# Hyperbolic attention as one program: projections and unit loop share one block, spike logits ride on v's projection, GpSimd spreads v

## The reference, cut to what matters

```python
importance = sigmoid(einsum('btc,c->bt', x, w_sur) + b_sur)
spikes = importance > threshold                    # one 0 or 1 for each token
q, k, v = x @ W_qkv + b_qkv
tq, sq = expmap0(q)    # nomin = sqrt(max(-u0^2 + sum(u[1:]^2), 1e-8)); cosh(nomin), sinh(nomin) u[1:] / nomin
tk, sk = expmap0(k)
neg_inner = tq tk^T - sq sk^T
dist = arccosh(max(neg_inner, 1 + 1e-7))
attn = softmax(causal(-dist**2 / sqrt(D))) * spikes
y = (attn @ v) @ W_out + b_out
```

## Time and profile before

| what | us |
|---|---|
| median of 3 runs (2066.55 to 2072.94) | 2069.12 |
| the profiled execution, whole | 2071.58 |
| its span, first to last instruction | 2069.8 |
| the stage's first instruction (ScalarE, L1703) starts | 1114.21 |
| the first unit's stretch starts | 1169.18 |
| the next stage's first instruction starts | 1286.41 |

### The profile page before, as it was taken

One profiled execution on the slowest core, in us unless ns is written; L12 is line 12 of the kernel. 1 busy time (PEld: TensorE's weight loads), 2 busy tenths in 40 slices (PEclk: granted clock), 3 DMA queues, 4 the chain that ended last, 5 costly groups with the idle time before them and its releaser, 6 DMA issues. The chain is left out here.

```text
span 2069.8 us, 35351 instructions
## 1 busy us (share of the span) xinstructions
PE 1923.5 (93%) x12240; PEld 1620.3 (78%) x12240; DVE 1434.9 (69%) x2398; ACT 1105.4 (53%) x2118; POOL 849.8 (41%) x854
## 2 busy tenths in 40 slices
PE   8999999999999999999998677999999768959998
PEld 6788888888888888888887465788799646849998
DVE  7777676767767676776776896433589577857776
ACT  6555555545555554555544697232355365636664
POOL 7350321405032140504200185220399225968885
PEclk9999999999999999999999799999999779969999
DMA  4101010010101001010102201310156215556661
GB/s 155 62 1 62 1 61 0 20 41 0 61 0 61 0 23 37 0 61 0 29 1 62 62 3 42 123 41 11 63 192 211 65 26 148 185 204 209 213 214 45
DMA packets 96322, 144.51 MB, mean 70 GB/s; under 512 B 15358, under 2 KB 72608, under 8 KB 96096
## 3 DMA queue, kind: packets, MB, share of 16 engines
q1 hardware_dynamic: 89168, 127.21, 19.1%
q0 software_dynamic: 4928, 12.86, 1.8%
q10 hardware_dynamic: 2128, 3.15, 0.4%
HBM read 111.46 MB, written 14.16 MB: 61 GB/s over the span
## 5 line engine op out<-in xcount | busy, mean ns | idle before, releaser
L319 PE MATMUL ps<-cond_x_lo,cond_w_hi 128*128 128x512 f32 x1008 | 392.6, 389 | 0.0
L471 ACT ACTIVATE cond_h_hi<-cond_h 128x512 fp32r<-128x512 f32 x288 | 174.0, 630 | 289.7 <-DVE cond_h L666 289.6
L805 POOL TENSOR_TENSOR cond_w_lo<-cond_stage_up,cond_w_hi 128x512 fp32r<-128x512 f32 x36 | 47.1, 1308 | 591.8 <-ACT cond_w_hi L471 591.8
L319 PE MATMUL ps<-cond_x_hi_first,cond_w_hi 128*128 128x512 f32 x578 | 230.1, 398 | 3.1 <-DVE ps L652 2.5
L382 PE MATMUL ps<-cond_h_hi,cond_d_hi 128*128 128x512 f32 x576 | 224.8, 390 | 4.1 <-DVE cond_h_lo L671 4.1
L319 PE MATMUL ps<-cond_x_hi_first,cond_w_lo 128*128 128x512 f32 x578 | 225.2, 390 | 0.0
L382 PE MATMUL ps<-cond_h_hi,cond_d_lo 128*128 128x512 f32 x576 | 224.3, 389 | 0.0
L382 PE MATMUL ps<-cond_h_lo,cond_d_hi 128*128 128x512 f32 x576 | 224.2, 389 | 0.0
L319 PEld LDWEIGHTS ps<-cond_x_lo,cond_w_hi 128*128 128x128 f32 x1008 | 189.3, 188 | 37.2
L649 DVE TENSOR_TENSOR ps<-cond_p_row,ps 128x512 f32<-128x512 f32 x142 | 98.7, 695 | 170.7 <-PE ps L319 170.7
L524 ACT ACTIVATE cond_h<-ps 128x512 f32<-128x512 f32 x216 | 124.7, 596 | 164.8 <-DVE cond_h_lo L671 132.2
(11 more groups left out here) (427 smaller groups left out, 5122.4 us busy)
## 6 DMA issues: line engine op xcount, KB each, us to landing
moe_stage_up<-in_L_ffn_expert_wv SPq DMA_DIRECT2D x22, 1024.0 KB, 7.9
typed_stage_up<-in_L_cond_wi SPq DMA_DIRECT2D x11, 1024.0 KB, 5.0
typed_stage_dn<-in_L_cond_wo SPq DMA_DIRECT2D x11, 1024.0 KB
moe_stage_dn<-in_L_ffn_expert_proj SPq DMA_DIRECT2D x11, 1024.0 KB
cond_stage_up<-in_L_cond_Wg SPq DMA_DIRECT2D x7, 1024.0 KB, 5.1
cond_stage_up<-in_L_cond_Wu SPq DMA_DIRECT2D x7, 1024.0 KB, 7.2
cond_stage_dn<-in_L_cond_Wd SPq DMA_DIRECT2D x7, 1024.0 KB, 9.5
rope_v_now<-rope_v_blk SPq DMA_DIRECT2D x16, 272.0 KB, 2.4
```

Of the source, the lines that this page charges most:

```text
L319: ins = pe.matmul(bank, ws[:, j, u, w], xs.rearrange("p o n -> p (o n)"), start=(opens and k == 0), stop=(k == 2), skip_group_check=True)
L471: copy = lambda dst, src: act.activation(dst, src, ACT.Copy)
L805: return pool.tensor_tensor(w_lo[:, j, :, A11:A12 + 1], raw_up[:, :, :, upper(j)], w_hi[:, j, :, A11:A12 + 1], ALU.subtract)
```

## The change

The two programs become one block in `hyper_attention`; `hyper_units` is gone.

- The loop over the 16 projections now runs, behind the projection of block `i`, the loop's step `i - 11` (`DELAY` = `FIRST` + 4 = 11) on TensorE, ScalarE and VectorE. So steps 0 to 4 stand among the projections of blocks 11 to 15, and the loop goes on at step 5 (`AFTER`) behind them.
- The chain of the map's factors is computed for 7 blocks (`FIRST`, parts behind blocks 7 to 10) and for 9 (its parts behind the last projection and in steps 5 and 6; its exponentials on ScalarE behind step 5). The reciprocal is gone: the factors scale the features 1 to 15 of each head, and the time part is written as half a cosh.
- `stretch` scales in place, 480 columns instead of 512, by GpSimd for units 0 to 6 and by VectorE from unit 7 on.
- `block_values`, the spreading of v, goes from ScalarE to GpSimd: a multiplication by a column of ones and zeros (tile 0 and 1 ahead of the first unit, tile 2 in steps 1 and 2, tile 3 behind the phases of steps 5 and 6).
- The spike weight vector is appended, twice, to v's weights, and its bias to v's bias, so v's projection has 258 columns and the 256 small matmuls are gone. Each tile's logits get their exponential on ScalarE; the rest runs in step 6; then SP moves the spikes from token order to unit order with 8 transfers of 32 x 8 single floats. The first division (unit 0, step 8) waits for them.
- The first source tile is rounded and split in pieces of 128 and 384 tokens.
- Buffers are laid over one another: the rounded source over the residual's place, so the residual is loaded behind the last projection; the squares, the masked distances, the probabilities and y over others.

The diff, cut to its core (the phases that only change their names or places are left out):

```diff
-            self.bias, self.bo, self.ws = sb("bias", [P, 2 * D]), sb("bo", [P, KC]), sb("ws", [P, KC])
-            self.vb = sb("vb", [P, D])
+            self.bias, self.bo = sb("bias", [P, 2 * D]), sb("bo", [P, KC])
+            self.vb = sb("vb", [P, D + 2])
...
+        if b_qkv is not None:
+            self.loads += [(self.wq[:, :, 3 * D + j], col(w_sur)) for j in range(2)]
...
+                sp.wait_ge(v_done, NP)
+                sp.dma_start(resT[:].rearrange("p c n -> p (c n)"), m.x_saved).then_inc(m.x_back, 16)
+                sp.wait_ge(sp_steps, 3)
+                for q in range(2):
+                    for sq in range(4):
+                        row = sq % 2 * T + q * S
+                        sp.dma_start(spike[sq * S:(sq + 1) * S].rearrange("p (i q) -> p i q", q=2)[:, :, q],
+                                     sig[row:row + S].rearrange("p (i a) -> p i a", a=2)[:, :, sq // 2],
+                                     allow_slow_non_contiguous=True).then_inc(spike_moved, 16)
...
+                def unit_steps(u):
+                    units(u, (out, 9), (mix, 8), (score, 3), (p_turn, 7), (y_turn, 8), (turn, 1))
...
+                for i in range(NP):
+                    project(i)
+                    unit_steps(i - DELAY)
+                for u in late_steps:
+                    unit_steps(u)
...
+                for u_step in late_steps:
+                    unit_steps(u_step)
+                    if u_step == AFTER:
+                        exponentials(1)
...
+                space_norm(NP - 1)
+                norms(1, 0)
+                for u_step in late_steps:
+                    unit_steps(u_step)
+                    if u_step == AFTER:
+                        norms(1, 1)
+                        norms(1, 2)
+                    elif u_step == AFTER + 1:
+                        norms(1, 3)
+                        spikes()
...
-                        ins = act.activation(vo, vi, ACT.Copy, scale=half2[:, h:h + 1])
+                    ins = pool.tensor_scalar(vo, vi, half2[:, h:h + 1], None, ALU.mult)
...
+                for tt in range(TT - 2):
+                    for h in range(2):
+                        block_values(tt, h)
+                for u_step in range(0, AFTER):
+                    unit_steps(u_step)
+                    if u_step in (1, 2):
+                        block_values(TT - 2, u_step - 1)
+                pool.wait_ge(src_ready, TT + 1)
+                pool.memset(prob[:, 0, :, S:], 0.0).then_inc(cleared, 1)
+                for u_step in late_steps:
+                    unit_steps(u_step)
+                    if u_step in (AFTER, AFTER + 1):
+                        block_values(TT - 1, u_step - AFTER)
```

More of the change, by code:

```diff
@@ L1360, in hyper_units @@
     causal = [m.const[:, at:at + n].unsqueeze(1).to_broadcast([P, H, n]) for at, n in zip((C_FIRST, C_SECOND), keys)]
[L1361 to L1367, removed]
-    sem = StageSemaphores(nc, tag)
-    stretched, turned, k_turned, q_taken, k_blocked = (
-        sem(n) for n in ("stretched", "turned", "k_turned", "q_taken", "k_blocked"))
+    sem = StageSemaphores(nc, tag)
+    src_rounded, src_ready = sem("src_rounded"), sem("src_ready")
+    qk_done, v_done, qk_taken, v_taken = sem("qk_done"), sem("v_done"), sem("qk_taken"), sem("v_taken")
+    v_doubled, v_blocked, ones_set = [sem(f"v_doubled{i}") for i in range(2)], sem("v_blocked"), sem("ones_set")
+    sp_small, sp_steps, spike_moved = (sem(n) for n in ("spike_exp", "spike_steps", "spike_moved"))
+    squared, made, norm_act, norm, spaced = (sem(n) for n in ("squared", "made", "norm_act", "norm_steps", "spaced"))
+    bias_joined = sem("bias_joined")
+    stretched = [sem(f"stretched{i}") for i in range(2)]
+    turned, k_turned, q_taken, k_blocked = (sem(n) for n in ("turned", "k_turned", "q_taken", "k_blocked"))
     scored, clamped, root_squared, root_logged, rooted = (
@@ new lines, in _ @@
+                for n, piece in enumerate(pieces[0:3]):
+                    split_src(n, *piece)
+                for i in range(NP):
+                    dve.wait_ge(qk_done, i + 1)
+                    dve.tensor_tensor(qk[:, i], qk_ps[i % 2], bias[:, 0:QK], ALU.add).then_inc(qk_taken, 1)
+                    if i >= 1:
+                        space_norm(i - 1)
+                    if FIRST <= i < FIRST + 4:
+                        norms(0, i - FIRST)
+                    if i % SUB == SUB - 1 and i // SUB + 2 < TT:
+                        split_src(i // SUB + 3, *pieces[i // SUB + 3])
+                    unit_steps(i - DELAY)
@@ L1599, in shift, with unit_steps @@
                                        ALU.subtract).then_inc(shifted, 1)
+                def unit_steps(u):
+                    units(u, (stretch, 0), (mask, 5), (root_add, 4), (shift, 5))
+                column = v_blk[:].rearrange("p i j g h v -> p (i j g) h v")[:, :, :, DH]
+                pool.tensor_copy(column, half2.unsqueeze(1).to_broadcast([P, NP * 2 * HP, 2])).then_inc(ones_set, 1)
+                for tt in range(TT - 2):
+                    for h in range(2):
+                        block_values(tt, h)
```

508 lines of the change are left out of this document (239 added, 269 removed).

## The result

| | before | after |
|---|---|---|
| median, us (range, runs) | 2069.0 (2066.6 to 2072.9, 4) | 2089.5 (2084.7 to 2093.6, 4) |
| the profiled execution's span | 2069.8 | 2091.8 |
| the stage's first instruction | 1114.2 | 1125.0 |
| the next stage's first instruction on ScalarE | 1286.4 | 1305.4 |
| the stage, start to start | 172.2 | 180.4 |

The ratio is 1.0097, with a 95% interval of 1.0078 to 1.0116: slower by some 20 us. The forecast was 2070.2 in a range of 2057 to 2084.

The account below looks back on a forecast made before the run. VectorE's work and waits were taken to bound the fill up to unit 1's maximum, ScalarE the full loop. −1.4 and −10.0, +11.6 for the lock and +0.9 behind gave +1.1: 2070.2 us, range 2057 to 2084, its own 2063 to 2076.

Parts of the forecast that it names:

- At nothing: Items priced at zero: the 256 spike matmuls, two more columns on v, the weights, the residual's load.
- VectorE's idle time: VectorE's waits ahead of the end of unit 1's maximum: kept at 9.0 us, bounds 6 and 12.
- last rival: Projections queue on TensorE behind turns waiting for GpSimd's stretch, so blocks 12 to 15 come late: +9, 2079; chance 0.05.
- Work that leaves VectorE: Ahead of unit 1's maximum: stretches 5.6, reciprocals 3.5, time parts 0.9, together −10.0 us.
- the lock: Two-input instructions of VectorE and GpSimd run in turn, each whole, delaying VectorE's chain: 4.1, 1.5 and 6.0, sum +11.6 us.
- One spreading, b = 2.2: One spreading of v on GpSimd, 1024 elements: 2.2 us, twice the COPY row, between bounds 0.96 and 4.9.
- line-rate rival: GpSimd spreads v as fast as a memset of the same size, b = 1.0: 2063.7 us; chance 0.16.
- The start: TensorE starts sooner behind ScalarE's first rounding because the first piece is smaller: 2.46 becomes 1.1, −1.4 us.
- The mark and behind it: The mark is the end of unit 1's maximum; behind it the last spreading delays mask 2, +0.9 us after slack.
- Spike transfers: Rival: the eight spike transfers land late and unit 0's division waits, about 2081 us; chance 0.08.
- slow spreading: Rival: GpSimd's spreading takes b = 4.9, deciding from about 3, holding stretches and chain: some +21, 2090 us; chance 0.11.
- The lock bites little: Rival: chain links slip between GpSimd's instructions, or GpSimd is late and idle, so +11.6 falls away: 2058.7 us; chance 0.22.

Follow-up runs that it names:

- e1: The changed kernel with 64 unused bytes behind the stage's weights, so the first stage's buffers lie 256 bytes further than before; 2078.3 us.
- e2: The kernel before with 192 unused bytes behind the stage's weights, so the first stage's buffers lie where the changed kernel has them; 2081.4 us.
- e3: The changed kernel with tile 2's two spreadings of v on GpSimd behind steps 3 and 4 instead of 1 and 2; 2087.1 us.
- e4: The changed kernel with both edits of e1 and e3: the 64 bytes and the later spreadings of tile 2; 2076.0 us.
- e11: e9 with the first seven stretches back on VectorE; 2068.7 us.
- e8: The kernel before with only v's eight spreadings moved from ScalarE to GpSimd; 2074.5 us, ratio 1.0027.
- e5: e4 with v's eight spreadings back on ScalarE, placed behind blocks 7 to 15 and steps 6 to 8; 2067.8 us, ratio 0.9997.
- e9: e5 with the spike instructions in step 5, ahead of the chain part awaiting exponentials, and ScalarE's last three spreadings behind step 5; 2061.2 us, ratio 0.9958.

## Why the prediction was wrong

**"At nothing: ... two more columns on v".** This step failed, and it is over half of the miss. As work the columns cost nothing, as predicted. As bytes they moved the first stage's buffers, and that costs 11.2 to 11.4 us (e1, e2). The prediction priced every instruction of the changed stage and asked nothing of what the allocation shifts. Without it the change measures 2078.3, inside the range of 2057 to 2084 but above the forecast's own.

**"VectorE's idle time: I keep 9.0, with bounds of 6 and 12."** It was 14.9. The clause "those of tile 2 were never waited for long" was wrong in the new order: in the kernel before ScalarE reached that spreading late; GpSimd, idle, reaches it 8.07 us early. The prediction had the chain of turn, stretch and projection in its last rival, at 0.05, and didn't put tile 2's transfer into it. e3 and e4 give 2.4 to 3.5 us back. The wait for the exponentials was there too, 2.7.

**Work that leaves VectorE, −10.0, and the lock, +11.6.** VectorE is busy for 45.7 where the two terms make 49.1. What links and spike instructions take above their undisturbed length adds up to 2.7 in the first group's chain (4.1 forecast), 1.9 in the second's first part (1.5) and 4.9 in step 6 (6.0), 9.5 in all. The step that was off is "they alternate, each whole". The rows of step 6 show `hyp_cosh` at 0.46 within GpSimd's 3.12, right behind a held link. The forecast came near because more was held per link and fewer links were. The stretches' term, 5.6, is 3.0 of the stage by e11; that the rest fell where VectorE waits anyway fits this, but wasn't shown by itself. The Trainium skill ("SBUF — State Buffer", section SBUF: two separate sides) has the lock held for the whole instruction; the earlier trace rows fit that, the links inside a spreading, in e8 above all, don't.

**One spreading, b = 2.2.** It is 2.9, 2.8 ns for each element, between the bounds and 0.7 above what was taken; ScalarE does the same in 1.14 to 1.22. The line-rate rival is refuted, and with it, for this instruction and stride, the Trainium skill's "roughly line-rate" for one input ("GPSIMD Engine Reference", section 4.1, Engine selection).

**The start, −1.4.** TensorE began 1.36 behind ScalarE instead of 2.46: −1.1. **The mark and behind it**: the mark moved by +4.1 (82.5 instead of 78.4), for +0.2 forecast. Behind it the forecast was 0.9 more, and this step failed too: unit 2's maximum was at +6.6 already. It stands behind the second spreading, and GpSimd's 1.3 of slack wasn't enough. To the last maximum it was +6.8, and the end moved by +8.2, because TensorE's clock fell to 0.50 in the last stretch; the prediction has no term for that. The period of the full loop stayed at 11.75 for two units, as said. **Spike transfers**: each landed 1.9 after its issue, and the first division waited for none; the rival is refuted.

The rivals: "slow spreading" (b from about 3) gave the right sign and nearly the time, 2090 for 2089.5, but by luck and another road; half of it was the addresses. "The lock bites little" is refuted by the 9.5 us that were held, and by e8's chain, 2.7 us longer. Spreading on GpSimd costs 5.1 us of the stage in this order (e5; the lock and GpSimd's own queue together) and 3.2 in the old one (e8). What the merged block is worth with v spread by ScalarE: as it stands (e5), no difference in the whole time, and 1.5 to 2.6 us at the last maximum; with its order mended (e9), 0.42% of the whole time, and 5.0 to 6.1 us there.

## What to carry to other kernels

Before pricing a change's work, ask what its buffers move: a few bytes in a tensor allocated early shift all behind it, and a stage that runs some 4800 matmuls back to back shows 2.4 ns in each; compare instruction counts in one full stretch of an untouched stage to see it, and put the shift back with a pad. An engine that is given a step because it is idle reaches it earlier, so a step that waits for a transfer must stand behind everything others wait for. Short instructions in a chain belong beside an engine's waits, and not beside a full GpSimd queue. Compare two profiles of a stage at a point inside it as well as at its end: here the end added up to 1.5 us where the clock was down.

## What the runs showed of the hardware

- TensorE's matmul of 512 columns came every 228.4 or 230.8 ns on average over 900 us, with the clock at 1.00 and TensorE busy throughout in both cases, by where its stage's buffers lie in SBUF; 64 bytes made the difference (after, e1). No single multiple is best in all stages; the rule is open.
- GpSimd's TENSOR_SCALAR with one pointer took 2.86 to 3.12 us for 128x1024 with a strided output.
- Beside GpSimd a VectorE instruction of 16 elements took 1.98 us instead of 0.17, while others of two inputs passed at their 0.42 to 0.46 us during a GpSimd spreading. Of its 2.9 us a spreading held two-input instructions back until 1.4 to 1.7 us behind its start, and not after (after, e8).
- Where the loop empties, TensorE's granted clock fell to 0.50 in some profiles and stayed full in others; the last part took 14.4 to 14.5 us at a mean clock of 0.83 to 0.88, 13.5 at 0.88 in e1, and 13.0 to 13.1 at 0.95 to 1.00.
